# Attention with grouped heads on TensorE: program written out, value products spread over the group

## The reference

```python
q = q * cos + rotate_half(q) * sin
k = k * cos + rotate_half(k) * sin
k = jnp.repeat(k, rep, axis=1)
v = jnp.repeat(v, rep, axis=1)
att = jnp.einsum('bhqd,bhkd->bhqk', q, k) * scale
att = jnp.where(causal, att, jnp.finfo(att.dtype).min)
att = jax.nn.softmax(att, axis=-1)
y = jnp.einsum('bhqk,bhkd->bhqd', att, v)
```

## Time and profile before

| | us |
|---|---|
| median of 3 runs | 1811.33 (1810.03 to 1817.43) |
| profiled execution | 1811.42 |
| its span | 1809.7 |
| TensorE busy in it | 1483.2 (82%) |
| ScalarE busy | 1159.0 (64%) |
| VectorE busy | 1263.2 (70%) |
| attention, first plain tile to last output | 231.8 to about 862 |

### The profile page before, as it was taken

The page is one execution under the profiler, slowest core; times in us unless marked ns, Lnnn a source line. Parts: engine busy times, 40 slices in busy tenths (PEclk is TensorE's granted clock), DMA queues, the critical chain, the costliest instruction groups (busy, mean ns, idle before and its releaser), DMA issues. The chain is left out here.

```text
span 1809.7 us, 41589 instructions
## 1 busy us (share of the span) xinstructions
PE 1483.2 (82%) x12722; PEld 1016.7 (56%) x12722; DVE 1263.2 (70%) x3160; ACT 1159.0 (64%) x2439; POOL 767.9 (42%) x1202
## 2 busy tenths in 40 slices
PE   3999568888888888887799269999977834999998
PEld 1455224434444444442355159999964524999997
DVE  3787367766767667771686657778768766777776
ACT  3788316666666566665588347877847623788775
POOL 2587714433434334442343446655302203665540
PEclk9999859999999999997899579999989866999998
DMA  5011221111111111100011311111001100111110
GB/s 143 24 55 53 79 61 36 37 31 35 36 36 37 32 35 36 38 15 1 12 36 35 105 28 40 38 30 29 22 1 31 41 24 21 52 49 45 51 39 23
DMA packets 84654, 71.14 MB, mean 39 GB/s; under 512 B 16753, under 2 KB 78001, under 8 KB 84529
## 3 DMA queue, kind: packets, MB, share of 16 engines
q1 hardware_dynamic: 76336, 52.62, 10.3%
q0 software_dynamic: 8192, 16.79, 3.5%
HBM read 46.81 MB, written 22.54 MB: 38 GB/s over the span
## 5 line engine op out<-in xcount | busy, mean ns | idle before, releaser
L1047 DVE TENSOR_REDUCE at_negmax<-at_s_ps 128x2 f32<-128x1024 f32 (+3 forms) x384 | 387.4, 1044 | 174.5 <-PE at_s_ps L830 174.3
L953 ACT ACTIVATE at_p<-at_x_ps 128x512 f32<-128x512 f32 x640 | 352.8, 596 | 149.9 <-PE at_x_ps L842 148.9
L1008 POOL TENSOR_SCALAR_AFFINE_SELECT at_p<-at_p 128x256 f32<-128x256 f32 (+1 forms) x448 | 189.8, 436 | 356.5 <-ACT at_p L953 356.4
L1269 POOL DMA_INDIRECT e_x_in<-xn,e_row_c x256 | 257.3, 1005 | 145.9 <-issue 76.6
L842 PE MATMUL at_x_ps<-at_qr,at_kr 50*128 50x512 bf16 (+3 forms) x1024 | 202.5, 308 | 76.0 <-ACT at_p L953 53.3
L1390 DVE TENSOR_TENSOR e_hid_lo<-e_hid,e_hid_hi 128x512 fp32r<-128x512 f32 x256 | 177.3, 693 | 83.2 <-ACT e_hid_hi L1354 73.4
L825 PE MATMUL at_s_ps<-at_kr,at_qr 48*128 48x512 bf16 (+3 forms) x1024 | 172.8, 317 | 44.8 <-DMA at_kr<-k_parts 20.8
L1353 ACT ACTIVATE e_hid<-e_h_ps 128x512 f32<-128x512 f32 x256 | 155.1, 606 | 41.5 <-PE e_h_ps L1295 37.0
L857 PE MATMUL at_o_ps<-at_p,at_va 128*32 128x512 f32 (+3 forms) x2048 | 170.4, 478 | 1.8 <-POOL at_p L1008 1.8
L1295 PE MATMUL e_h_ps<-e_x_hi,w_hi 128*128 128x256 f32 x512 | 156.2, 305 | 0.0
L1354 ACT ACTIVATE e_hid_hi<-e_h_ps 128x512 fp32r<-128x512 f32 x256 | 155.9, 609 | 0.0
(11 more groups left out here) (196 smaller groups left out, 3455.2 us busy)
## 6 DMA issues: line engine op xcount, KB each, us to landing
at_qr<-q_parts SPq DMA_DIRECT2D x128, 48.0 KB
at_kr<-k_parts SPq DMA_DIRECT2D x128, 48.0 KB
xres<-in_x_dram SPq DMA_DIRECT2D x8, 512.0 KB, 7.4
at_qr<-q_parts SPq DMA_DIRECT2D x128, 32.0 KB
xn<-m_n_xhat SPq DMA_DIRECT2D x16, 256.0 KB
e_x_in<-xn,e_row_c POOLq DMA_INDIRECT x256
xn<-sc_n_xhat SPq DMA_DIRECT2D x16, 256.0 KB
out_dram<-xres SPq DMA_DIRECT2D x16, 256.0 KB
```

Of the source, the lines that this page charges most:

```text
L953: a.activation(p_sb[g % 2][:, i, :], x_ps[i % 2][:], ACT.Exp, scale=SCALE).then_inc(x_read, 1)
L1008: sel = gp.affine_select(out=part, in_=part, compare_op=ALU.is_ge, fill=0.0, base=0, pattern=[[0, n] for n in part.shape[1:-1]] + [[1, P]] ...
L1047: v.tensor_reduce(out, scored, AX.X, ALU.max, negate=True).then_inc(s_read, 1)
L1269: nc.gpsimd.indirect_dma_start(out=x_in[k][u][:], out_offset=None, in_=xn_dram, in_offset=bass.IndirectOffsetOnAxis(ap=row_c[k][:, u:u + 1 ...
```

## The change

TensorE's program doesn't use `schedule` any more: all 16 batches are written out. The other engines keep their loop.

Value products are issued in three bursts a group instead of one, by the table WEIGH: chunk 0 behind tile 1, chunk 1 behind tile 4, chunks 2 and 3 behind tile 7. Each burst waits only for the masks that its chunks need. The row transpose goes from tile 2 to tile 4 (ROWS_AT), the misc work from tile 7 to tile 9, the copies of ScalarE and the splitting of GpSimd with them. A plain tile stands behind a shifted tile instead of before it, and begins on the other half of the rows. A group then goes X0 S0 X1 W0 X2 S1 X3 S2 X4 R W1 X5 S3 X6 S4 X7 W2 X8 S5 X9 M.

```diff
-S_BEFORE = {0: 0, 2: 1, 3: 2, 5: 3, 7: 4, 8: 5}
+S_AFTER = {0: 0, 2: 1, 3: 2, 5: 3, 6: 4, 8: 5}
-WEIGH_AT, MISC_AT = 2, 7
+WEIGH = {1: (0,), 4: (1,), 7: (2, 3)}
+ROWS_AT, OUTPUT_AT, MISC_AT, PARTS_AT = 4, 7, 9, 7
@@ TensorE, weigh
-                def weigh(n, u, g):
+                def weigh(n, u, g, chunks):
-                    if g == 0:
+                    if chunks[0] == 0 and g == 0:
                         pe.wait_ge(va_done, n + 1)
-                    if g % 2 == 0:
+                    if chunks[0] == 0 and g % 2 == 0:
                         after(pe, o_copied, n * NG + g // 2)
-                    pe.wait_ge(p_masked, (n * NKV + g) * 5 + 5)
-                    order = sorted((c, j, i, at) for i in range(NX) for c, j, at in X_TILES[i])
+                    order = sorted((c, j, i, at) for i in range(NX) for c, j, at in X_TILES[i] if c in chunks)
+                    masked = max(i // 2 for c, j, i, at in order) + 1
+                    pe.wait_ge(p_masked, (n * NKV + g) * 5 + masked)
...
-                    mm.then_inc(pv_done, 1)
+                    if chunks[-1] == 3:
+                        mm.then_inc(pv_done, 1)
@@ TensorE, step
-                            if ahead is not None and i in S_BEFORE:
-                                scores(*ahead, S_BEFORE[i], i % 2)
                             less_max(n, u, r, g, i)
-                            if i == WEIGH_AT and ahead_rows is not None:
+                            if ahead is not None and i in S_AFTER:
+                                scores(*ahead, S_AFTER[i], (i + 1) % 2)
+                            if i == ROWS_AT and ahead_rows is not None:
                                 max_rows(*ahead_rows, use(n, g, True))
-                            if i == WEIGH_AT and g:
-                                weigh(n, u, g - 1)
-                            elif i == WEIGH_AT and not is_first(n):
-                                weigh(n - 1, 1 - u, NKV - 1)
+                            if i in WEIGH and g:
+                                weigh(n, u, g - 1, WEIGH[i])
+                            elif i in WEIGH and not is_first(n):
+                                weigh(n - 1, 1 - u, NKV - 1, WEIGH[i])
@@ TensorE, all
-                schedule(pe, first, step, flush)
+                first()
+                for n in range(NB):
+                    step(n, n % 2, n // 2)
+                flush()
@@ ScalarE, step
-                            if i == WEIGH_AT and ahead_rows is not None:
+                            if i == 0 and g == 2 and not is_first(n):
+                                copy_normal(use(n, 1, False))
+                            if i == ROWS_AT and ahead_rows is not None:
                                 copy_rows(ahead_rows[0], ahead_rows[3], use(n, g, True))
-                            if i == WEIGH_AT and g == 0 and not is_first(n):
+                            if i == OUTPUT_AT and g == 0 and not is_first(n):
                                 copy_output(n - 1, 1)
-                            elif i == WEIGH_AT and g == 2:
+                            elif i == OUTPUT_AT and g == 2:
                                 copy_output(n, 0)
-                            if i == MISC_AT + 1 and g == 1 and not is_first(n):
-                                copy_normal(use(n, g, False))
@@ GpSimd, step
-                            if i == 5 and ahead_rows is not None:
+                            if i == PARTS_AT and ahead_rows is not None:
                                 max_parts(ahead_rows[0], ahead_rows[3], use(n, g, True))
```

More of the change, by code:

```diff
@@ L920, in flush @@
                     done = use(n, NKV - 1, False) + 1
-                    weigh(n, u, NKV - 1)
+                    for chunks in WEIGH.values():
+                        weigh(n, u, NKV - 1, chunks)
                     turn_output(n, 1, done)
```

## The result

| | us |
|---|---|
| before, median | 1810.68 (1809.29 to 1817.43, 4 runs) |
| after, median | 1705.0 (1701.66 to 1707.12, 4 runs) |
| ratio | 0.9408, 95% interval 0.9379 to 0.9436 |
| forecast | 1734, range 1718 to 1770 |

What follows compares the result with a forecast made beforehand. TensorE and ScalarE were taken to bound the kernel by waiting for each other in turns. From 1811.4 us: 26 off for edges, 57.5 for groups, 6 and 3 added, 3 off, giving 1734; range 1718 to 1770.

Steps and rivals of the forecast that it cites:

- take off 3 for the groups before and behind: Attention stage outside its 57 middle groups: 3 us saved at start and end together.
- 6 us for lateness: Added for lateness that a walk at best times leaves out: 0.1 us a group, 6 us.
- the 3 of straight code: TensorE's written-out program might slow 48 groups by 0.1 us each: bounds 0 and 5 us, 3 taken.
- the walk's 31.0 us a batch: Batch of four groups at 7.6 us, plus 0.5 for the output projection and 0.1 for copies: 31.0 us.
- The edges: Five back edges of TensorE's loop, removed by writing the program out: 5.2 us each, 26 us saved.
- rival 1: Other engines' loop edges appear, costing 5 x up to 3.3 us back: 1750 us, chance 6%.
- The walk through a group: One new group summed piece by piece, start to start on TensorE: 7.6 us; old order gives 8.5.
- The change of shape: TensorE's array switching into and out of value products, two more each way: 0.32 us in, 0.16 out.
- Rival 3: Bursts gain nothing, each added change of shape costing 0.5 us more than taken: 1785 us, chance 6%.
- exits: Leaving value products for other work: 0.16 us for each of two added exits, bounds 0 and 0.32.
- The copies: ScalarE's moved copies: copy_normal hidden in a gap; copy_output delays the next exponential some 0.2 us, counted 0.1 a batch.

## Why the prediction was wrong

The direction and both mechanisms of the steady groups were right. What failed are terms of the sum: "take off 3 for the groups before and behind", which measured 18.4 us of saving; the "6 us for lateness" and the 3 of straight code, which measured nothing; and the walk's 31.0 us a batch, which measured 30.47. Against 77.5 us in the sum stand 109.4 in the traces, 32 more (28 more by the medians).

- **The edges**, 26 us: 24.6 by putting the loop back. Right; of the 5.2 us an edge, what isn't stall goes with the clock: behind the stall at 441.94 it is 0.50 from 441.5 to 447.5 us, and value products take 3.95 us for 2.36, 1.6 more. That no other engine's edge would show, against rival 1, is right too. The 3.3 us an edge that the rival takes are the length of TensorE's own stalls; no run shows them for another engine, and the groups of after repeat to within 0.15 us. Of the two queues of instructions, q8 has 85 packets in before and with the loop put back, 72 in after and with the loop alone taken out; q14 has 40 or 41 in all four, and in after 7 from 290 to 360 us and none from there to 690, though the other engines go round their loops, as the earlier trace rows had none beside the 7 of the earlier trace rows. So q8 goes with TensorE's loop and q14 doesn't; which engines' instructions q14 brings, and whether late packets of q8 make the stall, no run shows.
- **The walk through a group**, 7.6: the group shown above sums to 7.61. Most pieces fall on the forecast: W0 to X2 1.00 (1.03), X2 to X4 1.07 (1.07), W1 to X5 0.78 (0.79), X5 to X7 1.08 (1.07), W2 to X8 0.79 (0.79), M to X0 0.58 (0.59). X9 to M is 0.45 (0.32), because this M waits for the output copy, and X0 to X1 0.36 (0.50). Two groups of four have neither this wait nor the projection and take 7.45. The walk missed 0.14 us in four X0-to-X1 steps a batch: the plain tile between them hides behind the shifted one more than I allowed. The reason that I gave for it, opposite halves of the rows, is not what does it: on the same half the step is 0.33. 31.0 a batch against 30.47, 7.5 us in 57 groups.
- **The change of shape**, the unknown price. The three bursts take 1.00 + 0.78 + 0.79 = 2.57 us to the next shifted tile, against 2.29 for the block: 0.14 for each of two more, forecast 0.16. Rival 3 is out: the bursts gain 64 us. The way back costs 0.14 us beyond the work. The way there lies in the 0.31 us from X1 to W0, of which a product of 512 columns takes 0.23 (S1 at 483.88 to its mask at 484.11, in the run with plain tiles first): 0.08 more, by estimate.
- **Lateness**, 6 us: there was none. A walk that starts each piece at the earliest moment already had the waits in it, as its check against the old order (8.5 for 8.49) had shown. The margin had no row behind it.
- **Straight code**, 3 us: none in the new order (7.45 with the loop and without). In the old order it does cost: 8.57 for 8.49, in three groups of four. Why there and not here stays open.
- **Start and end**, forecast 3 us, measured 18.4, half of the whole miss. I priced these groups by analogy and looked at neither their clock nor their length. The windows were there to be read: from 820 to 852 us, where before has no plain tiles, the granted clock is 0.79, 0.79, 0.57 and 0.71. Idle products in the place of the plain tiles held it at 1.00 to 844 us, and the end took 6 us less. In after the clock falls for one window of the groups only (0.79), and one burst in these groups alone brings 8 us back. What the other 7 us are, shorter groups and the order of the tiles among them, was not taken apart.

The range failed for the same reason: it reached 36 us towards the rivals and only 16 the other way, for its lower end took off lateness and exits and left the ends of the stage at 3 us. The lateness had no row behind it; the straight code had one, the batches of 35.27 us. The copies went as argued, though no run moved them alone: copy_normal stands in a gap, copy_output costs 0.2 us where M waits for it (7.65 for 7.45).

The five signs named in advance: no "issue" stall over 3 us, right; clock 1.00 from 300 to 700, right; records of W of 0.9, 0.7 and 0.7 us, missed by some 0.15 each (1.06, 0.85, 0.86); R to R of 7.6 to 7.8 with one of 8.1, too high by some 0.15 to 0.2 (7.45, 7.65, 7.46, 7.91); ScalarE's idle of 0.7, 0.7 and 0.5, too high by some 0.1 behind W0 and W1 (0.58, 0.57, 0.51).

## What to carry to other kernels

When two engines hand tiles to each other through two buffers, ask how long the longest piece of other work between two tiles is: here all but 0.42 us of it became idle time of the partner (from a block's start to the next shifted tile 1.00, 0.99 and, before the change, 2.73 us, for gaps of 0.58, 0.57 and 2.30), so that one block of 2.3 us cost more than three of 0.8 to 1.0 with two more changes of shape. Put what the partner waits for first behind each block, and other work behind that; with three blocks this order was worth 38 us. Price the first and the last turns of a pipeline by their own rows, their clock too.

## What the runs showed of the hardware

- TensorE's granted clock was at 1.00 or at half of that, 0.50, and fell though nothing stalled before: in the old order without the loop four groups ran value products in 3.9 to 4.1 us for 2.36, with TensorE 83 to 86% busy in the 10 us before. Idle products held it up at the end of the stage and made the kernel 0.26% quicker (0.03 to 0.48%).
- A back edge of TensorE's loop, around which queue q8 has 2 packets, cost it 2.5 to 3.8 us of stall and 1.5 to 2.8 more, with the clock at its lower level behind it: 4.2 to 5.4 in all in the new order, 5.2 to 5.7 in the old.
- Coming back from products on a quarter of the columns to products on half of the rows cost 0.14 us beyond the work: the same value products take 2.29 us in one burst, 1.00 + 1.43 in two and 2.57 in three.
- Whether a plain tile begins on the half of the rows that the shifted tile uses or on the other made no difference: 1704.8 and 1705.0 us.
